# Decoder block on one core: the gate's small tensors kept in the experts' PSUM bank, with a new order of steps

## The chip, the cores and the metric

The kernel runs on one core of one Trainium2 chip. The metric is the device time of one launch in microseconds; the median of the runs counts. A core has a matrix engine (PE, which the kernel calls tensor), and the engines DVE (vector), ACT (scalar), POOL (gpsimd) and SP (sync, here the queue that issues every DMA). Each works through its own instruction stream in order; semaphores tie the streams together.

## The reference, cut to what matters

For each of 32 batch entries (256 tokens of width 256) a pre-norm decoder block is computed: a causal self-attention with 8 heads that share one key and value (part a), a cross-attention with 16 heads, a bias per head and a mask (part b), and a mixture of 8 experts with a shared one (part c):

```
    x = x + _L0_attn_ref(_layernorm(x), Wq, Wk, Wv, Wo)
    x = x + _L0_xattn_ref(_layernorm(x), ctx, ctx, bias, bias, key_mask, attn_mask, ...)
    # part c, on the layer-normed x:
    logits = einsum('btd,ed->bte', x, gate_w)
    _, idx = top_k(logits + lb_bias, 2)
    w = sigmoid(take_along_axis(logits, idx))
    w = w / (sum(w) + 1e-6)                      # two weights per token
    hidden = square(relu(einsum('nd,ehd->neh', x, w1)))
    out = sum over e of w_e * (hidden_e @ w2_e)  + shared expert
```

The gate is the part from `logits` to the two weights per token. Its tensors are tiny: 128 partitions by 2 token tiles by 8 experts.

## The kernel before

Tokens lie on 128 partitions in CT = 2 tiles. Every float32 product is made of three float16 products (high and low parts), so each result of PE is split by ACT (high part) and by DVE or POOL (low part). The work of one batch entry is cut into named steps, and each engine has its own table of steps in `ORDERS`: an entry `c_gate:0@5` means step c_gate with argument 0, for the batch entry that is 5 behind the current iteration. `iterations` walks the table once for each of 32 + LAGS iterations, so parts a, b and c of up to four entries are under way at once, and the order of a table is the order of that engine's instructions. Only the order within an engine and the semaphores matter; where a table begins does not.

Steps that the text speaks of:
- b_s:j and b_p:j, head j of part b: PE makes the scores (L1089), DVE adds the bias and takes the maximum (L829), ACT takes the exponential (L663, L665) and the high part (L673), DVE makes the low part (L836), and SP transposes both with a DMA, b_pT:j (L422), for PE's b_pv:j (L1103).
- b_comb:j on POOL (L521) adds the mask to a bias tile of 128x512 in place; b_load:p on SP brings the bias of two heads (512 KB) into one of four slots, ahead by four.
- b_store_q, b_store_k, b_stack_q, b_stack_k on SP write the split queries and keys to memory and read them back stacked for PE (16 transfers of 64 KB); b_s:0 of the next entry waits for them.
- a_s, a_n, a_pt, a_pv, a_q, a_r: scores, scaling, transposes, values, queries and reciprocals of part a.
- b_wo and c_ln: end of part b (x2) and the layer norm of part c over DVE, POOL and ACT; c_T transposes its result on PE (L993) into ps_c_hidden.
- c_f1:e and c_f2:e, e from 0 (shared) to 8: first and second product of an expert, 12 matmuls each (L966). c_f1 writes the bank ps_c_hidden; POOL squares (L535) and makes the low part (c_lo, L542). c_f2 writes the bank ps_c_out, and DVE's c_f2:e adds it to acc (L929 for e = 0, L937 with the gate's weights for the others).
- c_gate: PE writes the 16 logit columns into ps_c_out (16 matmuls of 8 columns). ACT takes exp(-logits) (L685). DVE's chain has 13 parts and 19 counted instructions, L873 to L921, each waiting on the semaphore c_gd for the one before. All of its tensors after the first read lie in SBUF (g_logits, g_biased, g_mask1 and 2, g_exp1, g_w, g_sum1). PE's c_f2:0 waits for the first of the 19 alone, since only that one reads ps_c_out; DVE's c_f2:1 waits for all 19.

Of the kernel before, what the change touches and what calls it, by code (L numbers as in the profile page):

```python
# [66 lines left out]
def order(text):  # L67
# [31 lines left out]
        a_pv:1@3 b_s:1@4 a_s:6@3 w_split:10@3 b_p:0@4 c_T:0@5 a_pt:3@3 b_s:2@4 a_pv:2@3 b_p:1@4 b_s:3@4
        c_gate:0@5 c_gate:1@5 c_gate:2@5 a_s:7@3 c_gate:3@5 c_gate:4@5 c_gate:5@5 b_p:2@4 c_gate:6@5 a_pt:4@3  # L100
        w_split:11@3 c_gate:7@5 b_s:4@4 c_f2:0@5 c_gate:8@5 c_gate:9@5 b_p:3@4 c_gate:10@5 c_gate:11@5 a_r:6@3
        a_pv:3@3 b_s:5@4 c_gate:12@5 c_f2:1@5 a_r:7@3 a_pt:5@3 b_p:4@4 b_s:6@4 a_pv:4@3 b_p:5@4 c_f2:2@5
        a_pt:6@3 b_s:7@4 b_p:6@4 b_s:8@4 a_pv:5@3 w_split:12@3 c_f2:3@5 a_pt:7@3 w_split:13@3 b_p:7@4
        w_split:14@3 w_split:15@3 a_pv:6@3 b_s:9@4 a_pv:7@3 b_p:8@4 a_ln:0@2 b_s:10@4 b_p:9@4 c_f2:4@5 a_ln:1@2
        w_split:3@2 b_p:10@4 a_wo:0@3 b_s:11@4 b_ln:0@3 b_s:12@4 b_ln:1@3 b_p:11@4 c_f2:5@5 b_s:13@4 a_T:0@2
        b_p:12@4 b_T:0@3 b_mask:0@3 w_split:4@2 a_kv:0@2 b_s:14@4 w_split:5@2 b_p:13@4 a_q:0@2 w_split:6@2
        b_s:15@4 b_p:14@4 a_q:1@2 a_s:0@2 b_r:0@4 b_p:15@4 c_f2:6@5 a_r:0@2 a_s:1@2 b_kv:0@3 a_q:2@2 a_r:1@2
        a_s:2@2 a_pt:0@2 w_split:7@2 a_s:3@2 a_r:2@2 c_f2:7@5 b_n:0@4 a_q:3@2 a_pt:1@2 b_o:0@4 a_s:4@2 a_r:3@2
        w_split:8@2 c_f2:8@5 a_s:5@2 a_pv:0@2 b_wo:0@4 a_r:4@2 w_split:9@2 c_ln:0@4 a_r:5@2 c_ln:1@4 b_s:0@3
        a_pt:2@2""",  # L110
    tensor="""
        b_s:1@4 a_pt:3@3 c_T:0@5 b_s:2@4 a_pv:2@3 a_s:7@3 c_f1:0@5 a_pt:4@3 b_s:3@4 c_gate:0@5 c_f1:1@5 a_pv:3@3
        b_s:4@4 b_pv:0@4 c_f1:2@5 c_f2:0@5 c_f1:3@5 b_s:5@4 a_pt:5@3 c_f2:1@5 c_f1:4@5 b_s:6@4 a_pv:4@3 c_f2:2@5
        b_pv:1@4 b_pv:2@4 a_pt:6@3 c_f1:5@5 b_s:7@4 a_pv:5@3 b_pv:3@4 c_f2:3@5 b_s:8@4 c_f1:6@5 a_pt:7@3 b_s:9@4
        a_pv:6@3 b_pv:4@4 c_f2:4@5 a_pv:7@3 c_f1:7@5 b_s:10@4 a_wo:0@3 b_s:11@4 b_pv:5@4 c_f2:5@5 b_s:12@4
        a_T:0@2 c_f1:8@5 b_pv:6@4 b_s:13@4 b_pv:7@4 c_f2:6@5 b_s:14@4 b_T:0@3 a_kv:0@2 b_pv:8@4 b_q:0@3 a_q:0@2
        b_pv:9@4 b_s:15@4 b_kv:0@3 a_q:1@2 b_pv:10@4 b_pv:11@4 a_s:0@2 b_kv:1@3 b_pv:12@4 a_s:1@2 b_pv:13@4
        a_q:2@2 a_pt:0@2 a_s:2@2 c_f2:7@5 a_s:3@2 a_pt:1@2 b_pv:14@4 b_pv:15@4 a_q:3@2 b_o:0@4 a_s:4@2 a_pv:0@2
# [1111 lines left out]
```

## Time and profile before

| what | value |
|---|---|
| median of 3 runs | 2490.76 us (2489.09 to 2491.76) |
| the profiled execution, its own time | 2482.43 us |
| its span, first to last instruction | 2480.6 us |
| mean granted PE clock | 0.946 of full speed |
| busy share PE, DVE, ACT, POOL | 87%, 79%, 83%, 72% |

The profile is of one execution. Busy shares are averages over the whole span, and no engine is full; what ends a stretch is read from the stretch itself, with the windows, timeline and chain views below.

### The profile page before, as it was taken

How to read it: one execution, taken by the hardware profiler on the slowest of the kernel's cores; microseconds unless marked ns; L12 is line 12 of the kernel's file. 1: busy time of each engine (PE TensorE's matmuls, PEld its weight loads, DVE VectorE, ACT ScalarE, POOL GpSimd, SP SyncE). 2: the span in 40 equal slices, each digit the busy share in tenths (PEclk: the TensorE clock that was granted, in tenths of full speed). 3: DMA queues.
4: the chain of work that ended last, by engine and by line, in shares of the span. 5: the costliest groups of instructions: out<-in, count | busy, mean ns of one | idle time of the engine just before them, and what ended most of it. 6: DMA issues, size and time to landing. Idle time of an engine off the chain costs nothing.

```text
span 2480.6 us, 73034 instructions
## 1 busy us (share of the span) xinstructions
PE 2161.2 (87%) x24128; PEld 1852.2 (75%) x24128; DVE 1964.2 (79%) x6672; ACT 2070.0 (83%) x6065; POOL 1785.0 (72%) x1899
## 2 busy tenths in 40 slices
...
GB/s 155 121 166 153 160 144 152 147 150 154 163 149 141 148 148 163 153 157 137 140 153 171 146 166 143 147 144 165 155 163 155 146 139 149 166 148 160 137 131 35
DMA packets 711784, 367.16 MB, mean 148 GB/s; under 512 B 561392, under 2 KB 659952, under 8 KB 711408
## 3 DMA queue, kind: packets, MB, share of 16 engines
...
## 4 chain that ended last, share of the span: by engine, by line
PE 52%; DVE 17%; issue 12%; ACT 12%; DMA 4%; SPq 2%; POOL 1%; DVEq 0%; ACTq 0%; POOLq 0%
PE ps_a_misc L966 12%; PE ps_c_hidden L966 11%; PE ps_c_out L966 10%; DMA b_probsT_hi_lo<-b_probs_hi_lo 4%; PE ps_a_scores L1026 4%; PE ps_b_misc L1103 3%; DVE g_weights L921 3%; PE ps_a_misc L1045 3%; PE ps_b_scores L1089 3%; ACT ps_b_probs L665 2%; DVE b_neg_scores L829 2%; ACT ps_b_probs L663 2%; PE ps_b_misc L966 2%; ACT b_probs_hi_lo L673 1%; DVE g_mask L899 1%
## 5 line engine op out<-in xcount | busy, mean ns | idle before, releaser
L521 POOL TENSOR_TENSOR bias<-bias,b_mask 128x512 f32<-128x512 f32 x512 | 648.8, 1276 | 14.6 <-DMA bias<-in_bias 13.9
L542 POOL TENSOR_TENSOR c_hidden_lo<-c_hidden,c_hidden_hi 128x512 f16<-128x512 f32 x288 | 334.2, 1161 | 228.6 <-issue 207.0
L829 DVE CUSTOM_DVE_ANT_0 b_neg_scores<-ps_b_scores,bias 128x256 f32<-128x256 f32 x1024 | 390.0, 417 | 89.5 <-PE ps_b_scores L1089 83.5
L535 POOL TENSOR_TENSOR c_hidden<-c_relu 128x512 f32<-128x512 f32 x288 | 300.2, 1042 | 207.8 <-ACT c_relu L691 197.9
L836 DVE TENSOR_TENSOR b_probs_hi_lo<-ps_b_probs,b_probs_hi_lo 128x512 f16<-128x512 f32 x512 | 349.0, 682 | 126.9 <-ACT b_probs_hi_lo L673 119.1
L663 ACT ACTIVATE ps_b_probs<-b_neg_scores,b_neg_max 128x256 f32<-128x256 f32 x512 | 245.8, 480 | 200.7 <-DVE b_probs_hi_lo L836 133.3
L966 PE MATMUL ps_c_out<-w_hi,c_hidden_hi 128*128 128x256 f16 x1152 | 321.8, 279 | 92.6 <-DVE acc L937 90.2
L966 PE MATMUL ps_c_hidden<-c_xT_hi,w_hi 128*128 128x256 f16 x1152 | 326.3, 283 | 5.7 <-DVE c_xT_lo L744 4.6
L966 PE MATMUL ps_c_hidden<-c_xT_lo,w_hi 128*128 128x256 f16 x1152 | 324.5, 282 | 0.0
L966 PE MATMUL ps_c_out<-w_hi,c_hidden_lo 128*128 128x256 f16 x1152 | 324.4, 282 | 0.0
L966 PE MATMUL ps_c_out<-w_lo,c_hidden_hi 128*128 128x256 f16 x1152 | 323.5, 281 | 0.0
L966 PE MATMUL ps_c_hidden<-c_xT_hi,w_lo 128*128 128x256 f16 x1152 | 322.8, 280 | 0.0
L673 ACT ACTIVATE b_probs_hi_lo<-ps_b_probs 128x512 f16<-128x512 f32 x512 | 303.2, 592 | 4.9 <-DMA b_probsT_hi_lo<-b_probs_hi_lo 0.4
L937 DVE SCALAR_TENSOR_TENSOR acc<-ps_c_out,g_weights,acc 128x256 f32<-128x256 f32 x512 | 222.1, 475 | 34.7 <-PE ps_c_out L966 30.0
L665 ACT ACTIVATE ps_b_probs<-b_neg_scores,b_neg_max 128x256 f32<-128x256 f32 x512 | 239.5, 468 | 0.0
L1103 PE MATMUL ps_b_misc<-b_v_hi,b_probsT_hi_lo 128*128 128x16 f16 x4096 | 220.6, 170 | 12.8 <-DMA b_probsT_hi_lo<-b_probs_hi_lo 12.4
L1103 PEld LDWEIGHTS ps_b_misc<-b_v_hi,b_probsT_hi_lo 128*128 128x128 f16 x4096 | 205.3, 97 | 20.9 <-DMA b_probsT_hi_lo<-b_probs_hi_lo 15.5
L691 ACT ACTIVATE c_relu<-ps_c_hidden 128x512 f32<-128x512 f32 x288 | 172.4, 598 | 53.6 <-PE ps_c_hidden L966 50.3
L966 PEld LDWEIGHTS ps_c_out<-w_hi,c_hidden_hi 128*128 128x128 f16 x1152 | 114.5, 99 | 122.2 <-issue 104.3
L1103 PE MATMUL ps_b_misc<-b_v_lo,b_probsT_hi_lo 128*128 128x16 f16 x2048 | 195.9, 170 | 0.0
L696 ACT ACTIVATE c_hidden_hi<-c_relu 128x512 f16<-128x512 f32 x288 | 181.4, 630 | 1.4 <-PE ps_c_out L966 1.3
L479 POOL TENSOR_TENSOR a_qT_lo<-a_qT,a_qT_hi 128x512 f16<-128x512 f32 x128 | 150.4, 1175 | 42.7 <-ACT a_qT_hi L602 42.6
...
## 6 DMA issues: line engine op xcount, KB each, us to landing
bias<-in_bias SPq DMA_DIRECT2D x256, 512.0 KB, 4.3
q_stack<-qk_scratch SPq DMA_DIRECT2D x256, 64.0 KB, 3.6
...
k_stack_even<-qk_scratch SPq DMA_DIRECT2D x128, 64.0 KB, 3.6
```

Source lines behind the costliest of these rows:

```text
L521: gp.tensor_tensor(part, part, b_mask[:, :], ALU.add).then_inc(b_c_ok, 1)
L535: gp.tensor_tensor(c_h[:, :], c_r[:, e % 2, :], c_r[:, e % 2, :], ALU.mult).then_inc(c_sq_ok, 1)
L542: gp.tensor_tensor(c_hl[:, u, :], c_h[:, :], c_hh[:, u, :], ALU.subtract).then_inc(c_h_ok, 1)
L663: act.activation(ps_bp[:, 0:T], b_t[:, u, 0, :], ACT.Exp, bias=b_mx[:, u, 0:1], scale=-1.0, accum_out=b_sum[:, 0, j:j + 1])
L665: act.activation(ps_bp[:, T:2 * T], b_t[:, u, 1, :], ACT.Exp, bias=b_mx[:, u, 1:2], scale=-1.0, accum_out=b_sum[:, 1, j:j + 1]).then_inc(b ...
L673: act.activation(b_p2[:, j % DEPTH, :, 0, :], ps_bp[:, :].rearrange("p (c t) -> p c t", c=CT), ACT.Copy).then_inc(b_ph_ok, 1)
L696: act.activation(c_hh[:, e % 2, :], c_r[:, e % 2, :], ACT.Square).then_inc(c_hh_ok, 1)
L829: last = dve.tensor_tensor_reduce(out=b_t[:, u, c, :], in0=ps_bs[:, c * T:(c + 1) * T], in1=bias[:, slot, at:at + T], scale=-2.0, scalar=3 ...
L836: dve.tensor_tensor(b_p2[:, j % DEPTH, :, 1, :], ps_bp[:, :].rearrange("p (c t) -> p c t", c=CT), b_p2[:, j % DEPTH, :, 0, :], ALU.subtrac ...
L937: last = dve.scalar_tensor_tensor(out=acc[:, c, :], in0=ps_c2[:, c * D:(c + 1) * D], scalar=g_we[:, c, e - 1:e], in1=acc[:, c, :], op0=ALU ...
L966: last = pe.matmul(out, stat(s, k), mov(m, k), start=(k == 0 and n == 0), stop=(k == chunks - 1 and n == len(parts) - 1))
L1103: last = pe.matmul(ps_bm[:, at:at + BD], b_pT[:, u, c, part, s, :], v[:, s, j * BD:(j + 1) * BD], start=(s == 0 and n == 0), stop=(s == CT ...
```

## The change

Five of the gate's tensors move from SBUF into columns of ps_c_out behind the logits: exp1 (1 + exp), first and both (the masks), chosen (masks times sigmoid) and total (sum + 1e-6). The biased logits come straight from PSUM in one instruction in place of two, so GATE_STEPS goes from 19 to 18. No instruction of the gate on DVE then reads two tensors from SBUF, and the single-source ones on small tensors have their source or their result in PSUM, but for the cast of the indices. Since PE's c_f2:0 writes over that bank, it now waits for all 18 steps. All five tables of ORDERS are new.

```
-        GATE_STEPS = 19
+        GATE_STEPS = 18
...
+                logits, exp1, first, both, chosen = [
+                    ps_c2[:, n * CT * NE:(n + 1) * CT * NE].rearrange("p (c e) -> p c e", c=CT) for n in range(5)]
+                total = ps_c2[:, 5 * CT * NE:5 * CT * NE + CT]
...
-                    for c in range(CT):
-                        dve.tensor_tensor(g_sel[:, c, :], g_lg[:, c, :], lb[:, :], ALU.add).then_inc(c_gd, 1)
+                    dve.scalar_tensor_tensor(out=g_sel[:, :, :], in0=logits, scalar=1.0 / W_UP,
+                                             in1=lb[:, None, :].to_broadcast([P, CT, NE]), op0=ALU.mult,
+                                             op1=ALU.add).then_inc(c_gd, 1)
...
-                    dve.tensor_scalar(g_e1[:, :, :], g_ex[:, :, :], 1.0, None, ALU.add).then_inc(c_gd, 1)
+                    dve.tensor_scalar(exp1, g_ex[:, :, :], 1.0, None, ALU.add).then_inc(c_gd, 1)
...
-                        dve.tensor_scalar(g_m1[:, c, :], iota, g_idf[:, c, 0:1], None,
-                                          ALU.is_equal).then_inc(c_gd, 1)
+                        dve.tensor_scalar(first[:, c, :], iota, g_idf[:, c, 0:1], None, ALU.is_equal).then_inc(c_gd, 1)
...
-                    dve.tensor_tensor(g_w[:, :, :], g_m2[:, :, :], g_sg[:, :, :], ALU.mult).then_inc(c_gd, 1)
+                    dve.tensor_tensor(chosen, both, g_sg[:, :, :], ALU.mult).then_inc(c_gd, 1)
...
-                    dve.tensor_scalar(g_s1[:, :], g_s[:, :], 1e-6, None, ALU.add).then_inc(c_gd, 1)
+                    dve.tensor_scalar(total, g_s[:, :], 1e-6, None, ALU.add).then_inc(c_gd, 1)
...
-                        last = dve.tensor_scalar(g_we[:, c, :], g_w[:, c, :], g_si[:, c:c + 1], 1.0 / (W_UP * H_UP),
+                        last = dve.tensor_scalar(g_we[:, c, :], chosen[:, c, :], g_si[:, c:c + 1], 1.0 / (W_UP * H_UP),
...
                 if e == 0:
-                    pe.wait_ge(c_gd, after(b, GATE_STEPS, 1))
+                    pe.wait_ge(c_gd, after(b, GATE_STEPS, GATE_STEPS))
```

Of the tables, the lines of PE's after the change that hold its order from c_gate to c_f2:2:

```
+        b_s:0@3 b_s:1@3 a_pv:2@2 b_s:2@3 c_T:0@4 a_pt:4@2 b_s:3@3 c_f1:0@4 c_gate:0@4 a_pv:3@2 c_f1:1@4 b_s:4@3
+        b_pv:0@3 a_pt:5@2 c_f1:2@4 b_pv:1@3 b_s:5@3 a_pv:4@2 c_f1:3@4 a_pt:6@2 c_f2:0@4 b_s:6@3 c_f1:4@4
+        b_pv:2@3 a_pv:5@2 c_f2:1@4 b_s:7@3 c_f1:5@4 a_pt:7@2 c_f2:2@4 b_s:8@3 b_pv:3@3 a_pv:6@2 b_pv:4@3
```

In the table before, PE has c_f1:1, a_pv:3, b_s:4, b_pv:0 and c_f1:2 between c_gate:0 and c_f2:0. In the new one it has a_pv:3, c_f1:1, b_s:4, b_pv:0, a_pt:5, c_f1:2, b_pv:1, b_s:5, a_pv:4, c_f1:3 and a_pt:6.

The second half of the gate on DVE before the change; ps_b_scores, ps_b_probs and ps_a_misc belong to the attention parts, and the row of g_weights (L921) comes right behind these:

```order
L929 SCALAR_TENSOR_TENSOR acc<-ps_c_out,x 128x512
L908 TENSOR_TENSOR g_w<-g_mask,g_sigmoid 128x16
L911 TENSOR_REDUCE g_sum<-g_w 128x2
L836 TENSOR_TENSOR b_probs_hi_lo<-ps_b_probs,b_probs_hi_lo 128x2x256
L914 TENSOR_SCALAR g_sum<-g_sum 128x2
L917 RECIPROCAL g_inv<-g_sum 128x2
L799 RECIPROCAL a_inv<-a_sum 128x2
L774 TENSOR_TENSOR a_oT_lo<-ps_a_misc,a_oT_hi 128x256
L829 ISA b_neg_scores,b_neg_max<-ps_b_scores,bias 128x256
L829 ISA b_neg_max 128x1
L829 ISA b_neg_scores,b_neg_max<-ps_b_scores,bias 128x256
L829 ISA b_neg_max 128x1
```

The same place after the change:

```order
L909 TENSOR_REDUCE g_sum<-ps_c_out 128x2
L912 TENSOR_SCALAR ps_c_out<-g_sum 128x2
L915 RECIPROCAL g_inv<-ps_c_out 128x2
L794 RECIPROCAL a_inv<-a_sum 128x2
L919 TENSOR_SCALAR g_weights<-ps_c_out,g_inv 128x8 x2
L824 ISA b_neg_scores,b_neg_max<-ps_b_scores,bias 128x256
L824 ISA b_neg_max 128x1
L824 ISA b_neg_scores,b_neg_max<-ps_b_scores,bias 128x256
L824 ISA b_neg_max 128x1
L831 TENSOR_TENSOR b_probs_hi_lo<-ps_b_probs,b_probs_hi_lo 128x2x256
L927 SCALAR_TENSOR_TENSOR acc<-ps_c_out,x 128x512
```

The first accumulation (acc from ps_c_out and x) stood ahead of the gate's end and now stands behind it, and fewer attention steps stand between the gate's last parts.

SP at the end of a batch entry's part b, before the change, from the store of the queries on:

```order
L369 DMA bias<-in_bias 128x1024
L389 DMA qk_scratch<-b_qT_hi_lo 128x4x256
L422 DMA_TRANSPOSE b_probsT_hi_lo<-b_probs_hi_lo 128x8x128
L430 DMA key_padding<-in_pad 128x64
L382 DMA qk_scratch<-b_kT_hi_lo 128x4x256
L422 DMA_TRANSPOSE b_probsT_hi_lo<-b_probs_hi_lo 128x8x128
L414 DMA q_stack<-qk_scratch 16x8x256 x8
L403 DMA k_stack_even<-qk_scratch 16x8x256 x4
L403 DMA k_stack_odd<-qk_scratch 16x8x256 x4
```

The same place after the change:

```order
L384 DMA qk_scratch<-b_qT_hi_lo 128x4x256
L364 DMA bias<-in_bias 128x1024 x4
L417 DMA_TRANSPOSE b_probsT_hi_lo<-b_probs_hi_lo 128x8x128
L377 DMA qk_scratch<-b_kT_hi_lo 128x4x256
L417 DMA_TRANSPOSE b_probsT_hi_lo<-b_probs_hi_lo 128x8x128
L409 DMA q_stack<-qk_scratch 16x8x256 x8
L398 DMA k_stack_even<-qk_scratch 16x8x256 x4
L398 DMA k_stack_odd<-qk_scratch 16x8x256 x4
```

Four loads of bias (b_load:6, 7, 5 and 4) now stand together ahead of the last two transposes and the stacks, where one stood; the load of the padding row has gone elsewhere.

PE between the second head of part b and the second half of its fourth, around c_T, before the change:

```order
L1089 MATMUL ps_b_scores<-k_stack_odd,q_stack 128x256 x2
L1033 MATMUL ps_a_probsT<-constants,a_probs 128x128
L1034 MATMUL ps_a_probsT<-constants,a_probs 128x128
L1035 MATMUL ps_a_probsT<-constants,a_probs 128x128
L993 MATMUL ps_c_hidden<-constants,c_xn 128x128 x4
L1089 MATMUL ps_b_scores<-k_stack_even,q_stack 128x256 x2
```

And after it:

```order
L1087 MATMUL ps_b_scores<-k_stack_even,q_stack 128x256 x2
L991 MATMUL ps_c_hidden<-constants,c_xn 128x128 x4
L1031 MATMUL ps_a_probsT<-constants,a_probs 128x128
L1032 MATMUL ps_a_probsT<-constants,a_probs 128x128
L1033 MATMUL ps_a_probsT<-constants,a_probs 128x128
L1087 MATMUL ps_b_scores<-k_stack_odd,q_stack 128x256 x2
L964 MATMUL ps_c_hidden<-c_xT_hi,w_hi 128x256
```

Between c_T and the first expert product PE had b_s:2, a_pv:2 and a_s:7; now it has a_pt:4 and b_s:3 there.

## Rows read from the trace of the kernel before

**Rows 1.** The page: busy time, and the chain that ended last by engine.

```profile
PE 2161.2 (87%) x24128; PEld 1852.2 (75%) x24128; DVE 1964.2 (79%) x6672; ACT 2070.0 (83%) x6065; POOL 1785.0 (72%) x1899
...
PE 52%; DVE 17%; issue 12%; ACT 12%; DMA 4%; SPq 2%; POOL 1%; DVEq 0%; ACTq 0%; POOLq 0%
```

**Rows 2.** Windows: busy PE, PEld, DVE, ACT, POOL; PE clock; nine gate stretches, their sum.

```profile
1217.66:1227.66 10.00, 6.66 (x59) 5.21 (x58) 9.80 (x27) 6.73 (x22) 8.10 (x8) 1.00 0.32 68
...
sum 90.00, PE 59.58 PEld 46.44 DVE 87.81 ACT 60.52 POOL 72.84; mean PE 6.62 PEld 5.16 DVE 9.76 ACT 6.72 POOL 8.09
```

**Rows 3.** Timeline of DVE in one gate: start us, duration us, instruction.

```profile
1220.37 0.90 DVE L908 TENSOR_TENSOR g_w<-g_mask,g_sigmoid 128x16 f32<-128x16 f32 x1
...
1221.39 0.68 DVE L836 TENSOR_TENSOR b_probs_hi_lo<-ps_b_probs,b_probs_hi_lo 128x512 f16<-128x512 f32 x1
1221.99 0.51 DVE L914 TENSOR_SCALAR g_sum<-g_sum 128x2 f32<-128x2 f32 x1
...
1222.68 0.40 DVE L774 TENSOR_TENSOR a_oT_lo<-ps_a_misc,a_oT_hi 128x256 f16<-128x256 f32 x1
1223.00 0.41 DVE L829 CUSTOM_DVE_ANT_0 b_neg_scores<-ps_b_scores,bias 128x256 f32<-128x256 f32 x1
...
1223.68 2.27 DVE L921 TENSOR_SCALAR g_weights<-g_w,g_inv 128x8 f32<-128x8 f32 x2
```

**Rows 4.** Timeline of POOL in the same stretch.

```profile
1220.20 1.04 POOL L535 TENSOR_TENSOR c_hidden<-c_relu 128x512 f32<-128x512 f32 x1
1221.32 1.16 POOL L542 TENSOR_TENSOR c_hidden_lo<-c_hidden,c_hidden_hi 128x512 f16<-128x512 f32 x1
...
1224.66 1.26 POOL L521 TENSOR_TENSOR bias<-bias,b_mask 128x512 f32<-128x512 f32 x1
```

**Rows 5.** Groups of DVE's gate instructions: busy us, mean ns; last row min/median/max ns, first and last start.

```profile
L921 DVE TENSOR_SCALAR g_weights<-g_w,g_inv 128x8 f32<-128x8 f32 x64 | 69.8, 1133 | 0.0
L899 DVE TENSOR_SCALAR g_mask<-constants,g_idx_f 128x8 f32<-128x8 f32 x64 | 35.0, 590 | 0.0
L908 DVE TENSOR_TENSOR g_w<-g_mask,g_sigmoid 128x16 f32<-128x16 f32 x32 | 28.2, 881 | 0.0
L891 DVE TENSOR_SCALAR g_exp<-g_exp 128x16 f32<-128x16 f32 x32 | 19.5, 608 | 13.5 <-ACT g_exp L685 13.4
L914 DVE TENSOR_SCALAR g_sum<-g_sum 128x2 f32<-128x2 f32 x32 | 16.7, 522 | 0.0
...
L873 DVE TENSOR_SCALAR g_logits<-ps_c_out x32: 168/169/175, 177.0 to 2449.2; 128x16 f32<-128x16 f32 x32
```

**Rows 6.** The chain that ended last, pieces of PE: start us, us.

```profile
1195.71 0.49 PE ps_a_scores L1026 x6
...
1229.16 0.16 PE ps_a_probsT L1033
...
1229.54 1.31 PE ps_c_hidden L966 x12
1230.85 0.22 PE ps_b_scores L1089 x2
...
1231.57 0.28 PE ps_b_misc L1103 x12
```

**Rows 7.** Windows as in rows 2: stretches ahead of nine gates (12 us); one behind.

```profile
sum 108.00, PE 80.36 PEld 61.75 DVE 83.32 ACT 85.12 POOL 42.42; mean PE 8.93 PEld 6.86 DVE 9.26 ACT 9.46 POOL 4.71
...
1300.02:1322.02 22.00, 22.00 (x241) 19.51 (x239) 16.95 (x57) 18.93 (x53) 15.35 (x18) 0.92 0.77 156
```

**Rows 8.** Timelines of SP's queue and PE before a first head; the bias load's landing.

```profile
1258.38 0.57 SPq L369 DMA_DIRECT2D bias<-in_bias  x1
...
1264.42 3.95 SPq L414 DMA_DIRECT2D q_stack<-qk_scratch  x8
...
1276.08 0.38 PE L1089 MATMUL ps_b_scores<-k_stack_even,q_stack 128*128 128x256 f16 x2 [0.33 <-issue]
...
bias<-in_bias SPq DMA_DIRECT2D x256, 512.0 KB, 4.3
```

More of the change, by code:

```diff
@@ L81 @@
+        b_pT:7@4 b_pT:9@4 a_T:0@2 b_pT:10@4 b_pT:12@4 b_pT:11@4 b_pT:13@4 b_store_q:0@3 b_load:6@4 b_load:7@4
+        b_load:5@4 b_load:4@4 b_pT:14@4 b_store_k:0@3 b_pT:15@4 b_stack_q:0@3 b_stack_k:0@3 b_pT:0@3 b_load:0@3
+        b_pT:1@3 b_load:1@3 c_f2:8@5 b_pT:2@3""",
     gpsimd="""
-        b_v:0@4 b_comb:5@4 a_q:3@3 b_comb:6@4 c_ln:0@5 b_res:0@4 c_f1:0@5 c_lo:0@5 c_f1:1@5 c_lo:1@5 b_kv:0@3
-        c_f1:2@5 c_lo:2@5 b_comb:7@4 c_f1:3@5 b_comb:8@4 c_lo:3@5 b_comb:9@4 c_f1:4@5 c_lo:4@5 c_f1:5@5 c_lo:5@5
@@ L98 @@
-    vector="""
[L99 to L110, printed above, removed]
@@ L111 @@
-    tensor="""
[L112 to L118, printed above, removed]
-        c_f2:8@5 a_s:5@2 b_wo:0@4 a_pt:2@2 a_pv:1@2 a_s:6@2 b_s:0@3""",
+        c_ln:0@5 b_comb:2@4 b_comb:3@4 b_comb:4@4 b_v:0@4 b_comb:5@4 c_f1:0@5 b_res:0@4 c_lo:0@5 c_f1:1@5
```

89 lines of the change are left out of this document (50 added, 39 removed).

## The prediction, made before the changed kernel ran

> **What bounds the kernel now.** I read the page first. No engine is full: PE is busy 87% of the span, ACT 83%, DVE 79%, and the chain that ended last is 52% PE, 17% DVE, 12% ACT [rows 1]. So the bound changes from stretch to stretch. Counting the starts of the gate's first DVE instruction, 32 of them from 177.0 to 2449.2 us [rows 5], one batch entry takes (2449.2 - 177.0) / 31 = 73.3 us. I then cut nine entries by the windows view, each relative to that first instruction. In the ten microseconds from 4 to 14 us behind it the picture is the same in all nine: DVE is busy 9.76 of 10, while PE is busy 6.62, ACT 6.72 and POOL 8.09 [rows 2]. DVE alone bounds this stretch, and PE stands idle for 3.4 us and ACT for 3.3 us of it. Elsewhere PE bounds: it is busy all of 22.00 us in the stretch behind the gate shown in [rows 7]. Ahead of the gate there is another hole, which DVE does not fill either (PE busy 8.93 of 12, DVE 9.26, POOL 4.71 [rows 7]): there the layer norm c_ln goes round DVE, POOL and ACT.
>
> What fills DVE in the gate stretch are tiny instructions that take long. g_weights handles 8 columns in 1133 ns on average, while the read of the logits, 16 columns from PSUM, takes 169 ns [rows 5]. The timelines side by side say why. L908 ends at 1220.37 + 0.90 = 1221.27, and POOL's L535 had ended at 1221.24. L914 ends at 1222.50, POOL's L542 at 1222.48. The two of L921 end at 1225.95, POOL's L521 at 1225.92 [rows 3, 4]. Each of these waits until the running POOL instruction is over, and ends some 0.03 us behind it; meanwhile DVE's whole queue stands behind it. The instruction of 128x512 next to them, L836, reads one SBUF tensor and one PSUM tensor, and takes 0.68 us beside a busy POOL without any such stretch [rows 3].
>
> **What the change removes.** With 169 ns as the length of such an instruction when nothing holds it, the excess over 32 entries is: L921 69.8 - 64 x 0.17 = 58.9 us; L899 35.0 - 10.9 = 24.1; L908 28.2 - 5.4 = 22.8; L891 19.5 - 5.4 = 14.1; L914 16.7 - 5.4 = 11.3 [rows 5]. Together 131.2 us, or 4.1 us per entry. The instruction saved in the biased logits is one of that same small size. I call it nothing.
>
> Three of the five (L891, L899, L914) will read SBUF and write PSUM, and no DVE instruction of the trace does that. The bounds are 0.17 us as for the read from PSUM, and their present length, which would keep 24.1 + 14.1 + 11.3 = 49.5 us of the excess, 1.5 us per entry. I take the low end, since the row nearest to them (L873, the same operation with PSUM on the other side) has it. The Trainium skill ("VectorE: DVE Perf Modes", What auto-detection actually checks) says that the two-port mode is taken when the single source and the destination both lie in SBUF. No run here shows yet that a destination in PSUM is enough; by that rule the low end holds, and with the high end the forecast would be some 46 us later.
>
> The other two, and the reductions and masks, now read PSUM. The row for that is L873, 168 to 175 ns in all 32 [rows 5], so I price it at nothing. The Trainium skill ("VectorE: DVE Perf Modes", The TRN2 errata) gives a fixed part of 120 cycles from PSUM against 58 from SBUF at 0.96 GHz, 65 ns more each; for nine such reads that is an estimate of 0.6 us per entry, 18 us in all, and it speaks against this change. The forecast would be 2425 by it.
>
> **What it is worth.** DVE loses 4.1 us of work in a stretch where it was the bound by 3.3 us, the idle time of ACT, next after it. So 3.3 us is the most that this stretch gives per entry. POOL idles 1.9 us there and 7.3 us in the stretch ahead [rows 2, 7]; the new POOL order puts b_comb:1 to b_comb:5 ahead of the first expert's square, where it was idle, so I don't count it as a limit.
>
> **What it adds.** PE's c_f2:0 now waits for the whole gate. Behind it on PE stand b_s:6, c_f1:4 and everything that follows; ACT's c_sq:2, POOL's c_lo:2 and DVE's c_f2:0 wait for it in turn. On PE between c_gate and c_f2:0 lie, by [rows 6], three c_f1 at 1.31, two a_pv at 0.50 (1231.07 to 1231.57, between b_scores' end and b_misc), two a_pt at 0.38 (1229.16 to 1229.54), two b_s at 0.22, two b_pv at 0.3: 6.7 us. On DVE the 18 steps are at most 18 x 0.17 = 3.1 us when free, and between them stand two b_p at 0.60, one b_s at 0.68 (1223.00 to 1223.68), one a_pv at 0.32, one a_pt at no more than b_p's 0.60, two reciprocals at 0.17 [rows 3, 5]: 3.1 us, together 6.2 us. The wait is covered by 0.5 us. If the gate were still held by POOL, it would be 6.2 + 4.1 = 10.3 us against 6.7, a stall of 3.6 us for every engine, about as much as PE idles now.
>
> **What moves.** Between c_T and c_f1:0 PE had b_s, a_pv and a_s (0.22 + 0.50 + 0.49 [rows 6]) and has a_pt and b_s (0.38 + 0.22). The way from c_T through ACT and DVE is not shorter, so I charge 0.6 us of new idle time on PE. Ahead of b_s:0, where PE waits for the stacked keys, PE gets c_f2:6, a_pt:3 and a_s:7 and gives a_q:1 away: 1.31 + 0.38 + 0.5 - 1.31 = 0.9 us more cover. On SP three more bias loads stand ahead of the stacks. Their issue alone is 3 x 0.57 = 1.7 us; if each held the queues for its whole time to landing, it would be 3 x 4.3 = 12.9 us [rows 8]. Before, PE waited 0.33 us at this place in the entry shown. I take the issue end, since bias loads are issued throughout while other transfers land, and of it 0.9 is covered by PE; the rest of 0.8 I set against the fact that SP waits for b_p:14 anyway. Net nothing.
>
> **The sum.** 3.3 - 0.6 = 2.7 us per entry, times 31 periods = 84 us. The profiled execution took 2482.4 us (1.8 more than its span), so 2398 on its scale; the median of the runs stands 8.3 us above it, so 2407.
>
> **Rivals.**
> - More than that (15%). In [rows 7] the granted clock behind the gate is 0.92, with PE busy all the time, after PE's idle time in the gate. Six of nine entries showed 0.92 or 0.93 there, which costs 0.08 x 22 = 1.8 us each, 1.2 on average. If PE no longer idles, this goes too, and if the hole ahead of the gate does not grow: 3.3 + 1.2 = 4.5 us, 140 us, 2351.
> - Part of it is lost again (20%). The gate ends later than c_f2:0 by a microsecond, because exp(-logits) comes late from ACT or b_p waits inside the gate, or three of the five keep their length (1.5 us). Then 1 to 1.5 us per entry, 31 to 47 us: 2445 to 2460.
> - The change doesn't do what it says (5%). The instructions still wait for POOL, for another reason than two SBUF tensors. The stall is then at c_f2:0 instead of in DVE's queue, 3.6 against 3.4 us: 2490 to 2500. Against it: L836 beside a busy POOL.
> - Slower (10%), by one mechanism: the burst of bias loads makes the stacks late. It decides from the point where they come later than 2.7 us of gain plus 0.9 of cover, 3.6 us. With a delay halfway between 1.7 and 12.9, 7.3 us, the entry is 3.7 us longer, 115 us: about 2605; at 5 us it is 1.4 us, 2534. For it: the stacks are already what PE waits for. Against it: only 0.33 us.
>
> **How the numbers follow.** The forecast of 2407, with 2380 to 2440 around it, holds 50%. With 15% for more, 20% for less and 5% + 10% for the last two, faster by over 0.2% is 0.85, within 0.2% (about what this measurement can tell) 0.05, slower 0.10. The range of 2350 to 2470 takes in the forecast, most of the first rival and all of the second.
>
> **What would show it.** Right: g_weights' two near 0.2 us each and none of the gate's instructions ending with a POOL instruction; DVE under 9 of 10 us in the gate stretch and PE near full there; a period near 70.6 us; PE's idle time before c_f2:0 under 0.5 us. Wrong: PE idle before c_f2:0 for the gate's last step by more than 1 us, PE idle before b_s:0 for the stacks by more than 1.5 us, or the instructions that write PSUM still at 0.5 us or more.

## The result, and the profile after the change

The median went from 2490.76 to 2469.91 us (2468.02 to 2475.79 over five runs), a ratio of 0.9923 (95% interval 0.9907 to 0.994). Of the five runs of the kernel before, four took 2487.29 to 2491.76 us; one took 4171.51 us and is left out of the ratio. The change makes the kernel 21 us faster where 84 were forecast. The median lies just inside the upper end of the range, and that is luck: a gain that I had too small makes up for half of a loss that I had overlooked (see the part on why).

The page of the kernel after the change, busy time and chain, as in [rows 1]:

```profile
PE 2161.8 (88%) x24128; PEld 1865.0 (76%) x24128; DVE 1862.6 (75%) x6640; ACT 2078.2 (84%) x6065; POOL 1780.3 (72%) x1899
...
PE 59%; ACT 17%; DMA 10%; issue 7%; DVE 3%; SPq 3%; POOL 1%; ACTq 0%; DVEq 0%; POOLq 0%
```

DVE fell from 17% of the chain to 3%, and DMA rose from 4% to 10%. Where each happens, the windows show. Below are, after the change, the stretches from 24 to 13, from 13 to 1 us ahead of the gate's first DVE instruction and from 4 to 14 us behind it: the first of nine entries, then the sum of the nine (columns as in [rows 2]; PE's clock is the third number from the end).

```profile
380.12:391.12 11.00, 7.46 (x77) 6.48 (x76) 6.04 (x22) 5.79 (x19) 6.65 (x6) 0.84 1.26 151
...
sum 99.00, PE 70.23 PEld 59.09 DVE 49.91 ACT 48.49 POOL 51.39; mean PE 7.80 PEld 6.57 DVE 5.55 ACT 5.39 POOL 5.71
391.12:403.12 12.00, 8.88 (x69) 6.61 (x68) 10.75 (x41) 11.78 (x40) 7.27 (x9) 0.86 0.51 62
...
sum 108.00, PE 74.35 PEld 53.76 DVE 91.80 ACT 101.97 POOL 64.10; mean PE 8.26 PEld 5.97 DVE 10.20 ACT 11.33 POOL 7.12
408.12:418.12 10.00, 9.97 (x114) 8.90 (x112) 8.82 (x32) 9.87 (x28) 8.98 (x8) 1.00 0.73 149
...
sum 90.00, PE 89.77 PEld 79.88 DVE 78.50 ACT 88.60 POOL 81.18; mean PE 9.97 PEld 8.88 DVE 8.72 ACT 9.84 POOL 9.02
```

The last of the three answers to [rows 2]: PE 9.97 of 10 in place of 6.62. The first is new. Before the change these 11 us were full:

```profile
sum 99.00, PE 96.07 PEld 86.11 DVE 84.26 ACT 90.85 POOL 89.60; mean PE 10.67 PEld 9.57 DVE 9.36 ACT 10.09 POOL 9.96
```

Now every engine idles there together, PE for 3.2 us, ACT for 5.6, DVE for 5.5, and the granted clock (a mean over the window), 1.00 in all nine before, was 0.69 in seven of nine. What they wait for stands in the groups of PE's matmuls (by form; the last number is PE's idle time ahead of the group over the whole span, with its releasers), first before the change, then after:

```profile
L966 PE MATMUL ps_c_hidden<-c_xT_hi,w_hi 128*128 128x256 f16 x1152 | 326.3, 283 | 5.7 <-DVE c_xT_lo L744 4.6 <-ACT c_relu L691 1.2
L966 PE MATMUL ps_c_out<-w_hi,c_hidden_hi 128*128 128x256 f16 x1152 | 321.8, 279 | 92.6 <-DVE acc L937 90.2 <-POOL c_hidden_lo L542 1.4 <-DVE acc L929 0.6
L1103 PE MATMUL ps_b_misc<-b_v_hi,b_probsT_hi_lo 128*128 128x16 f16 x4096 | 220.6, 170 | 12.8 <-DMA b_probsT_hi_lo<-b_probs_hi_lo 12.4
L1089 PE MATMUL ps_b_scores<-k_stack_even,q_stack 128*128 128x256 f16 x512 | 104.0, 287 | 42.2 <-issue 23.8 <-DVE b_neg_max L829 18.3
L1089 PE MATMUL ps_b_scores<-k_stack_odd,q_stack 128*128 128x256 f16 x512 | 100.0, 277 | 56.2 <-DVE b_neg_max L829 56.1
```

```profile
L964 PE MATMUL ps_c_hidden<-c_xT_hi,w_hi 128*128 128x256 f16 x1152 | 326.3, 283 | 32.2 <-DVE c_xT_lo L739 27.4 <-ACT c_relu L686 3.7
L964 PE MATMUL ps_c_out<-w_hi,c_hidden_hi 128*128 128x256 f16 x1152 | 318.9, 277 | 9.7 <-POOL c_hidden_lo L537 4.6 <-DVE acc L935 3.6
L1101 PE MATMUL ps_b_misc<-b_v_hi,b_probsT_hi_lo 128*128 128x16 f16 x4096 | 225.6, 170 | 107.6 <-DMA b_probsT_hi_lo<-b_probs_hi_lo 107.4
L1087 PE MATMUL ps_b_scores<-k_stack_odd,q_stack 128*128 128x256 f16 x512 | 102.7, 284 | 43.7 <-DVE b_neg_max L824 43.6
L1087 PE MATMUL ps_b_scores<-k_stack_even,q_stack 128*128 128x256 f16 x512 | 99.4, 276 | 19.8 <-DVE b_neg_max L824 14.9 <-issue 4.8
```

PE's busy time plus its idle time is the span, so these rows make a ledger that closes. The third column is experiment e4 below; "rest" is the span less the lines above it.

| us over the span | before | after | e4 |
|---|---|---|---|
| PE busy | 2161.2 | 2161.8 | 2112.7 |
| idle before c_f2 (ps_c_out) | 92.6 | 9.7 | 9.1 |
| idle before b_pv (ps_b_misc) | 12.8 | 107.6 | 8.8 |
| idle before b_s, both parities | 98.4 | 63.5 | 64.5 |
| idle before c_T | 35.8 | 32.5 | 31.9 |
| idle before c_f1's first product | 5.7 | 32.2 | 31.3 |
| rest | 74.1 | 60.3 | 60.4 |
| span | 2480.6 | 2467.6 | 2318.7 |

The change took 82.9 us from the wait before c_f2 and 34.9 from those before b_s, and gave 94.8 us to the wait of b_pv for its transposed probabilities, which had been no wait to speak of, and 26.5 to c_f1's first product. A row tells where PE waits, and not which part of the change moved it; e2 below shows that for the first of them. The landing times (page, DMA issues: KB each, median us) of the loads and of the store of the keys that stands between the last two transposes:

```profile
bias<-in_bias SPq DMA_DIRECT2D x256, 512.0 KB, 4.7
...
qk_scratch<-b_kT_hi_lo SPq DMA_DIRECT2D x32, 256.0 KB, 6.7
```

That store took 3.7 us before, now 6.7. One such place on SP's queue, and the wait on PE behind it (timelines; for PE the bracket is the idle time and its releaser):

```profile
1247.43 3.42 SPq L364 DMA_DIRECT2D bias<-in_bias  x4
1250.95 1.46 SPq L417 DMA_TRANSPOSE b_probsT_hi_lo<-b_probs_hi_lo  x1
1252.54 0.69 SPq L377 DMA_DIRECT2D qk_scratch<-b_kT_hi_lo  x1
1253.33 3.68 SPq L417 DMA_TRANSPOSE b_probsT_hi_lo<-b_probs_hi_lo  x1
...
1260.36 0.19 PE L1101 MATMUL ps_b_misc<-b_v_hi,b_probsT_hi_lo 128*128 128x16 f16 x1 [2.12 <-DMA b_probsT_hi_lo<-b_probs_hi_lo]
```

The last transpose is issued at 1253.33 and its matmuls start at 1260.36, 7 us later. The four loads ahead of it bring 2 MB. The three transposes issued from 1245 to 1266 us took 6.8 us to land (median); in like stretches of e4 and e9 below it is 3.7 and 3.4 us.

### The profile page after: what moved, and what is told of

Its sections match the earlier page's. It is cut to its first block, busy times and chain, and to the rows that moved or that the text cites. A ratio compares the mean times of both kernels' runs of the same rounds, so it can differ in the third digit from the quotient of the medians.

```text
span 2467.6 us, 73004 instructions
## 1 busy us (share of the span) xinstructions
PE 2161.8 (88%) x24128; PEld 1865.0 (76%) x24128; DVE 1862.6 (75%) x6640; ACT 2078.2 (84%) x6065; POOL 1780.3 (72%) x1899
## 2 busy tenths in 40 slices
DMA packets 711784, 367.16 MB, mean 149 GB/s; under 512 B 561392, under 2 KB 659952, under 8 KB 711408
## 4 chain that ended last, share of the span: by engine, by line
PE 59%; ACT 17%; DMA 10%; issue 7%; DVE 3%; SPq 3%; POOL 1%; ACTq 0%; DVEq 0%; POOLq 0%
PE ps_c_hidden L964 18%; PE ps_c_out L964 13%; PE ps_a_misc L964 11%; DMA b_probsT_hi_lo<-b_probs_hi_lo 10%; PE ps_b_misc L1101 4%; PE ps_b_scores L1087 3%; ACT ps_b_probs L658 3%; PE ps_a_misc L1043 3%; ACT ps_b_probs L660 2%; PE ps_a_scores L1024 2%; PE ps_a_misc L1044 1%; ACT b_probs_hi_lo L668 1%; ACT a_probs L603 1%; SPq L417 1%; ACT c_xn L569 1%
## 5 line engine op out<-in xcount | busy, mean ns | idle before, releaser
L964 PE MATMUL ps_c_hidden<-c_xT_hi,w_hi 128*128 128x256 f16 x1152 | 326.3, 283 | 32.2 <-DVE c_xT_lo L739 27.4
L530 POOL TENSOR_TENSOR c_hidden<-c_relu 128x512 f32<-128x512 f32 x288 | 300.0, 1042 | 73.4 <-ACT c_relu L686 58.8
L1101 PE MATMUL ps_b_misc<-b_v_hi,b_probsT_hi_lo 128*128 128x16 f16 x4096 | 225.6, 170 | 107.6 <-DMA b_probsT_hi_lo<-b_probs_hi_lo 107.4
L964 PE MATMUL ps_c_out<-w_lo,c_hidden_hi 128*128 128x256 f16 x1152 | 317.8, 276 | 0.0
L964 PE MATMUL ps_c_out<-w_hi,c_hidden_lo 128*128 128x256 f16 x1152 | 317.5, 276 | 0.0
L618 ACT ACTIVATE a_probsT_hi<-ps_a_probsT 128x384 f16<-128x384 f32 x256 | 126.4, 494 | 144.4 <-PE ps_a_probsT L1033 144.3
L454 POOL TENSOR_TENSOR c_ve<-c_mv,eps 128x2 f32<-128x2 f32 x32 | 6.2, 194 | 280.3 <-DVE c_mv L732 280.3
```

The lines of the kernel that those rows point to most:

```text
L530: gp.tensor_tensor(c_h[:, :], c_r[:, e % 2, :], c_r[:, e % 2, :], ALU.mult).then_inc(c_sq_ok, 1)
L964: last = pe.matmul(out, stat(s, k), mov(m, k), start=(k == 0 and n == 0), stop=(k == chunks - 1 and n == len(parts) - 1))
L1101: last = pe.matmul(ps_bm[:, at:at + BD], b_pT[:, u, c, part, s, :], v[:, s, j * BD:(j + 1) * BD], start=(s == 0 and n == 0), stop=(s == CT ...
```

## The experiments

All times are medians; "before" was run again on each chip: 2484.63 us for e1 to e4, 2486.35 for e5 to e8, 2486.82 for e9. With the 2490.76 us above it differs by 6 us from chip to chip, so a difference between runs of two chips is good to about that; e1 to e4 compare best with each other, and so do e5 to e8.

**e1: the four loads spread out.** The changed kernel, SP's table alone edited:

```
- a_ln:0@3 b_pT:8@4 b_pT:7@4 b_pT:9@4 a_T:0@2 ... b_pT:11@4 b_pT:13@4 b_store_q:0@3
- b_load:6@4 b_load:7@4 b_load:5@4 b_load:4@4 b_pT:14@4
+ a_ln:0@3 b_load:4@4 b_pT:8@4 b_pT:7@4 b_pT:9@4 b_load:5@4 a_T:0@2 ... b_pT:11@4 b_load:6@4 b_pT:13@4
+ b_store_q:0@3 b_load:7@4 b_pT:14@4
```

> The changed kernel with one edit: on SP, b_load:4, 5 and 6 stand between the transposes b_pT:6 and b_pT:13 again, so that one bias load instead of four stands ahead of the last two transposes. The changed kernel lost 2.7 us of PE time per entry in the 11 us that begin 24 us ahead of the gate, behind transposes that took 6.8 us (median of the three in that stretch) to land. Theory 1, the burst of four loads makes those transposes late: they land in about 4 us, the hole closes by 2 to 3.5 us per entry, and the time falls by 60 to 110 us, to 2360 to 2410. Theory 2, PE, ACT and DVE simply reach the last heads in an order that leaves no cover for a transpose, whatever else is loaded: the hole stays at 2 us or more and the time at 2455 to 2475. Theory 3, moving the loads back delays the transposes in the middle of the entry instead: PE waits there, and the time stays within 20 us of 2470.

Measured 2339.04 us, ratio 0.9411 [0.939, 0.9433]: 131 us below the changed kernel, more than the 60 to 110 of theory 1. PE's wait for the transposes fell from 107.6 to 18.9 us. The burst is the cause, and it cost more than I gave it.

**e2: the gate of before with the new tables.** The five tensors back in SBUF, c_f2:0 waiting for one step again; all tables as after the change.

> The gate as before the change (all its tensors in SBUF, 19 steps, PE's c_f2:0 waiting for the first of them alone) with the new tables of steps. If the moved tensors saved 3.3 us per entry in the gate stretch and the new tables cost the rest, this kernel has the loss without the gain: 2470 + 31 x 3 to 3.5 = 2560 to 2580. If the new tables alone would have hidden the slow gate (DVE has less beside it there), it stays within 30 us of 2470. The long instructions (g_weights 1.1 us) should be back in both cases, and PE's wait of about 3.5 us is then for DVE's c_f2:0.

Measured 2539.35 us, 1.0229 [1.0205, 1.0254]: 55 us slower than before and 69 us slower than the whole change. So the new tables alone lose, and the gate's edit is worth 69 us beside them. Neither theory had this number; it lies between them. The groups of PE:

```profile
L966 PE MATMUL ps_c_out<-w_hi,c_hidden_hi 128*128 128x256 f16 x1152 | 319.2, 277 | 6.0 <-DVE acc L937 3.8 <-POOL c_hidden_lo L542 2.3
L1103 PE MATMUL ps_b_misc<-b_v_hi,b_probsT_hi_lo 128*128 128x16 f16 x4096 | 225.5, 170 | 107.1 <-DMA b_probsT_hi_lo<-b_probs_hi_lo 106.8
```

The wait for the transposes is all there (107.1 us) without the new gate. The wait before c_f2 is gone too (6.0 us), which the last sentence of the expectation had wrong: with the slow gate in the new tables, PE waits for DVE before a_pt (45.0 us, 4.0 in the changed kernel) and b_s (86.7 us, there 63.5) instead. So the row of c_f2 in the ledger is the tables' doing, and the gate's worth is read from the spans: PE's idle time is 374.9 us here and 305.8 in the changed kernel, 69.1 less, at the same busy time.

**e3: the new gate with the tables of before.** In DVE's table c_gate:12 goes ahead of a_r:6 and c_f2:0 behind b_s:5, so that c_f2:0 stands behind the gate's end; in PE's, three more steps lie ahead of c_f2:0:

```
DVE + c_gate:11 c_gate:12 a_r:6 a_pv:3 b_s:5 c_f2:0 c_f2:1
PE  - c_f1:2 c_f2:0 c_f1:3 b_s:5 a_pt:5 c_f2:1 c_f1:4
PE  + c_f1:2 c_f1:3 b_s:5 a_pt:5 c_f2:0 c_f1:4 c_f2:1
```

> The gate in PSUM, 18 steps, with the tables of before. DVE's c_gate:12 goes ahead of b_s:5 and its c_f2:0 behind it, and on PE c_f2:0 and c_f2:1 go two and one expert products later, since c_f2:0 has to wait for the whole gate. Theory 1 (the gate's gain is whole, the new tables lost most of it on SP): 3.3 us less per entry, less up to 1 us for c_f2:0 reached after 5.5 us of PE work with 6 us of gate on DVE: 2 to 3.3 us per entry, 2390 to 2430. Theory 2 (any order gives the gain back, since PE then arrives earlier at transfers that take as long as before): 2455 to 2480.

Measured 2485.42 us, 0.9994 [0.9973, 1.0015]: no difference from before. Theory 1 missed by 55 us or more. Theory 2 missed by 5, and its reason is not what happened: PE's wait for the transposes (13.8 us) and the part of b_s's wait without a releaser (27.4) stayed near those of before (12.8 and 23.8). DVE was relieved (5.63 of 10 us in the gate stretch), but PE rose only to 7.17. Its groups show why:

```profile
L963 PE MATMUL ps_c_hidden<-c_xT_hi,w_hi 128*128 128x256 f16 x1152 | 325.8, 283 | 74.0 <-ACT c_relu L685 71.1 <-DVE c_xT_lo L738 2.9
L963 PE MATMUL ps_c_out<-w_hi,c_hidden_hi 128*128 128x256 f16 x1152 | 315.5, 274 | 68.0 <-DVE g_weights L918 36.9 <-DVE acc L934 27.9 <-POOL c_hidden_lo L536 2.0
```

c_f2:0 now waits for g_weights (36.9 us), and ACT's c_sq:2, which waits for that same product, holds ACT's c_relu late, for which c_f1 waits in turn: 71.1 us, where it was 1.2.

**e4: two loads among the transposes, two behind the stacks.** As e1, but

```
- b_pT:11@4 b_load:6@4 b_pT:13@4 b_store_q:0@3 b_load:7@4 b_pT:14@4 b_store_k:0@3 b_pT:15@4
+ b_pT:11@4 b_pT:13@4 b_store_q:0@3 b_pT:14@4 b_store_k:0@3 b_pT:15@4
- b_stack_q:0@3 b_stack_k:0@3 b_pT:0@3
+ b_stack_q:0@3 b_stack_k:0@3 b_load:6@4 b_load:7@4 b_pT:0@3
```

> As e1_loads_spread, but b_load:6 and b_load:7 go behind the 16 stack transfers, so that no bias load stands between b_store_q and the last two transposes. Theory 1 makes the transposes faster still: 0 to 20 us below e1_loads_spread. If the loads are then too late for POOL's b_comb:4 of the next entry, POOL waits for them, and it is slower than e1_loads_spread.

Measured 2318.93 us (2315.76 to 2320.98), 0.9337 [0.9319, 0.9356]. This version beats both kernels, by 166 us the one before and by 151 us the changed one, and e1 by 20, the most that was expected. Its chain by engine:

```profile
PE 77%; ACT 12%; issue 7%; DVE 2%; DMA 1%; POOL 1%; SPq 0%; ACTq 0%; DVEq 0%; POOLq 0%
```

The stretch from 24 to 13 us ahead of nine gates, windows as above:

```profile
sum 99.00, PE 98.79 PEld 89.70 DVE 88.80 ACT 95.25 POOL 90.24; mean PE 10.98 PEld 9.97 DVE 9.87 ACT 10.58 POOL 10.03
```

And the group of b_pv:

```profile
L1101 PE MATMUL ps_b_misc<-b_v_hi,b_probsT_hi_lo 128*128 128x16 f16 x4096 | 220.0, 170 | 8.8 <-DMA b_probsT_hi_lo<-b_probs_hi_lo 8.8
```

The hole is closed, the clock there is 1.00 in all nine, and the ledger says where the 148.9 us between the two spans come from: 98.8 from b_pv's wait, 49.1 from PE's busy time, the rest from elsewhere. The 49.1 us are the same 24128 matmuls at a mean granted clock of 0.960 instead of 0.938 (2161.8 x 0.938 / 0.960 = 2112.3, measured 2112.7).

**e5: the kernel before, with three loads together.** The same fault put into the kernel before the change:

```
- b_load:7@5 b_store_q:0@4 b_pT:14@5
+ b_store_q:0@4 b_load:6@5 b_load:7@5 b_load:5@5 b_pT:14@5
```

b_load:5 and b_load:6 are taken from their places among b_pT:8 to b_pT:12.

> The kernel before with one edit on SP: b_load:5 and b_load:6 move from the middle of the entry to between b_store_q and b_pT:14, beside b_load:7, so three bias loads stand together ahead of the last two transposes (b_load:4 can't join them in these tables, since POOL would wait for it ahead of the queries that SP waits for). If loads standing together are what costs, this alone makes the kernel before slower: with four of them the changed kernel lost 2.7 us of PE and more by the clock per entry, and spreading three of them gave back 131 us. Here PE reaches the last heads later relative to their transposes, so less: 30 to 100 us above 2485. If the burst costs only together with the new order on PE, within 15 us of 2485.

Measured 2588.69 us, 1.0415 [1.0389, 1.044]: 102 us slower, just above the 30 to 100 expected. PE's wait for the transposes rose from 12.8 to

```profile
L1103 PE MATMUL ps_b_misc<-b_v_hi,b_probsT_hi_lo 128*128 128x16 f16 x4096 | 223.7, 171 | 96.3 <-DMA b_probsT_hi_lo<-b_probs_hi_lo 96.0
```

so three loads do it nearly as well as four, with no other part of the change present. The keys' store lands 5.8 us after its issue here, where it was 3.7.

**e6: e4 with the gate of before.**

> The kernel of e4_loads_last_two_behind_stacks with the gate of before (SBUF, 19 steps, c_f2:0 waiting for the first). Measured against it, this is the worth of the gate in tables whose SP order does no harm. If the gate's worth is the 2.2 to 3.3 us per entry of the gate stretch whatever SP does: 2319 + 68 to 105 = 2387 to 2424. If the slow gate is worth less once SP's hole is gone (something else then ends the entry): under 2370. If it is worth more, since PE's idle time also lowers its clock: over 2430.

Measured 2407.74 us, 0.9686 [0.9659, 0.9713]: 88.8 us above e4, 2.9 us for each of 31 periods, inside the 68 to 105 expected. This is the gate's worth with the burst out of the way. By the profiled spans (2414.8 and 2318.7 us) the difference is 56.8 us of PE's idle time, 1.8 per period, and 39.3 of its busy time (2152.0 against 2112.7), at a mean granted clock of 0.946 against 0.960. As in e2, the wait is not where it was before the change: c_f2 waits only 8.0 us, and the steps that share DVE's queue with the gate wait instead.

```profile
L1033 PE MATMUL ps_a_probsT<-constants,a_probs 128*128 128x128 f32 x256 | 77.5, 303 | 21.5 <-DVE a_probsT_lo L767 20.3 <-ACT a_probs L617 1.3
...
L1045 PE MATMUL ps_a_misc<-a_probsT_hi,a_v_hi 128*128 128x256 f16 x256 | 72.1, 282 | 37.3 <-DVE a_oT_lo L774 36.0
```

**e7: e4 with the layer norm c_ln ahead of b_p:0 on ACT.** The hole just ahead of the gate is left in e4 (PE 8.60 of 12).

```
ACT - w_split:11@2 b_p:0@3 c_ln:0@4 a_pv:2@2 b_s:1@3 c_T:0@4 b_p:1@3
ACT + w_split:11@2 c_ln:0@4 b_p:0@3 a_pv:2@2 c_T:0@4 b_s:1@3 b_p:1@3
```

> The kernel of e4_loads_last_two_behind_stacks with two edits in ACT's table: c_ln:0 ahead of b_p:0, and c_T:0 ahead of b_s:1. In its trace c_ln started 1.1 us after POOL's last step for it, behind b_p:0, and PE stood idle for 0.94 us ahead of c_T and 1.08 us ahead of the first expert product. If ACT's order is what PE waits for there: 0.5 to 1.2 us less per entry, 2282 to 2304. If b_p:0, which is then later, or the scores of the second head take over the wait: 2310 to 2335.

Measured 2326.56 us, 0.9352 [0.9325, 0.9379]: no gain over e4, from which it can't be told (8 us above it, with intervals that overlap). The first theory fell; the second, that b_p:0 or the scores of the second head take over the wait, gave 2310 to 2335, and the groups bear it out:

```profile
L964 PE MATMUL ps_c_hidden<-c_xT_hi,w_hi 128*128 128x256 f16 x1152 | 328.4, 285 | 17.2 <-DVE c_xT_lo L739 13.4 <-ACT c_relu L686 3.8
L1087 PE MATMUL ps_b_scores<-k_stack_odd,q_stack 128*128 128x256 f16 x512 | 103.9, 287 | 84.8 <-DVE b_neg_max L824 84.8
L991 PE MATMUL ps_c_hidden<-constants,c_xn 128*128 128x128 f32 x128 | 24.5, 322 | 13.7 <-ACT c_xn L569 13.6
```

Against e4's 31.3, 44.1 and 31.9, the two waits that c_ln causes lost 32 us together, and the wait of the odd heads for b_neg_max gained 41. Putting one of two urgent steps of ACT first only changes which of them PE waits for.

**e8: e3 with ACT's c_sq:2 later,** from behind b_p:3 to behind a_pt:5, where the product that it needs is due:

```
ACT - b_p:3@3 c_sq:2@4 c_f1:3@4 a_s:7@2 b_s:4@3 a_pt:5@2 b_p:4@3
ACT + b_p:3@3 c_f1:3@4 a_s:7@2 b_s:4@3 a_pt:5@2 c_sq:2@4 b_p:4@3
```

> The kernel of e3_new_gate_old_orders (new gate, tables of before) with one edit in ACT's table: c_sq:2 goes from behind b_p:3 to behind a_pt:5, since it waits for c_f2:0, which now waits for the whole gate; in its trace ACT stood idle for 3.1 us on it, with a relu and two heads behind it that PE needed. If the gain of the new gate was lost to this queue behind the new wait: 1 to 3 us per entry less, 2390 to 2455. If PE's own wait for the gate's last step (1.2 us in that trace) and the later c_f2 chain are what took it: within 20 us of 2485.

Measured 2434.53 us, 0.9784 [0.9758, 0.9809]: one step moved on one engine gives 51 us. The wait for c_relu fell:

```profile
L963 PE MATMUL ps_c_hidden<-c_xT_hi,w_hi 128*128 128x256 f16 x1152 | 322.1, 280 | 34.3 <-ACT c_relu L685 30.4 <-DVE c_xT_lo L738 3.9
```

That is inside the 2390 to 2455 expected. c_f2's own wait stayed (67.4 us). In the new tables it is 9.7 us, with more work between c_gate and c_f2:0; that such work alone would take it away in the old ones too was not run.

**e9: the changed kernel with loads of a quarter.** SP's order is untouched; b_load:4 to 7 bring 256 of the 1024 columns, and the rest of those bias tiles is left out.

```
- sp.dma_start(bias[:, p % SLOTS, :], bias_d[b * PAIRS + q])
+ sp.dma_start(bias[:, p % SLOTS, 0:256], bias_d[b * PAIRS + q][:, 0:256])
```

> The changed kernel, its order untouched, with the four bias loads that stand together (b_load:4 to 7) each bringing 256 of 1024 columns, 128 KB in place of 512 KB. It leaves out the rest of those loads, so half of the heads use stale bias values. The number of transfers and SP's instructions are the same. If it is the bytes in front of the last two transposes that make them late, the hole closes as it did when the loads were spread: 2470 less 90 to 160 us, 2310 to 2380. If it is SP's time to issue four more transfers (some 2.5 us for the four), or the waits ahead of them in SP's queue, the time stays above 2430.

Measured 2320.15 us, 0.9323 [0.9298, 0.9349]: 150 us below the changed kernel, the same as e4, with every DMA issued in the same place of the queue. PE's wait for the transposes:

```profile
L1101 PE MATMUL ps_b_misc<-b_v_hi,b_probsT_hi_lo 128*128 128x16 f16 x4096 | 220.0, 170 | 9.4 <-DMA b_probsT_hi_lo<-b_probs_hi_lo 9.3
```

SP's timeline at such a place:

```profile
1246.73 2.90 SPq L364 DMA_DIRECT2D bias<-in_bias  x4
1249.73 1.25 SPq L417 DMA_TRANSPOSE b_probsT_hi_lo<-b_probs_hi_lo  x1
...
1251.90 1.29 SPq L417 DMA_TRANSPOSE b_probsT_hi_lo<-b_probs_hi_lo  x1
```

The four loads still take 2.90 us to issue, where the full ones took 3.42, and of the two transposes behind them the first takes 1.25 in place of 1.46, the last 1.29 in place of 3.68. It is the bytes ahead of the transposes, not SP's time to issue the loads, nor the order as such. The fewer bytes over the whole run (318.40 MB in place of 367.16) are no rival: e4 moves all of them and is as fast.

## Why the prediction was right in direction and wrong in size

**The total: two errors that partly cancel.** Without the burst the change gains 166 us (e4), twice the forecast of 84; the burst takes some 150 of them back (151 between e4 and the changed kernel), for which the forecast had nothing.

**What the change removes: right.** The five groups priced at 131.2 us of excess went from 169.2 us of busy time [rows 5] to 38.8, 130.4 less. DVE's whole busy time fell by less, 101.6, since others grew, the cast by 7.5 us and b_mask by 6.4 among them. After the change, DVE's groups:

```profile
L919 DVE TENSOR_SCALAR g_weights<-ps_c_out,g_inv 128x8 f32<-128x8 f32 x64 | 11.5, 222 | 0.1
L898 DVE TENSOR_SCALAR ps_c_out<-constants,g_idx_f 128x8 f32<-128x8 f32 x64 | 11.3, 222 | 0.0
L906 DVE TENSOR_TENSOR ps_c_out<-ps_c_out,g_sigmoid 128x16 f32<-128x16 f32 x32 | 5.6, 173 | 0.0
L912 DVE TENSOR_SCALAR ps_c_out<-g_sum 128x2 f32<-128x2 f32 x32 | 5.2, 164 | 1.1
L890 DVE TENSOR_SCALAR ps_c_out<-g_exp 128x16 f32<-128x16 f32 x32 | 5.2, 162 | 0.0
```

A result in PSUM is enough: L912 and L890 read SBUF and write PSUM in 0.16 us, the low end that I took. The added reads from PSUM cost nothing that shows: L906 takes 173 ns, and the same operations, from SBUF before and from PSUM now, took 170 and 165 (the sum), 165 and 171 (the reciprocal g_inv), 246 and 245 ns (the reciprocal g_sigmoid). So the 65 ns more for each that the Trainium skill ("VectorE: DVE Perf Modes", The TRN2 errata) would give, which had the forecast at 2425, do not appear in these rows.

**What it is worth: right, a little less.** "3.3 us is the most": measured 2.9 us per period with the rest of the tables good (e6 against e4), 2.2 (69 us) beside the burst (e2). But the 3.3 were meant as idle time, and of the 2.9 some 1.8 are; the rest is busy time, most of it by the clock (2152.0 x 0.946 / 0.960 = 2120.6, measured 2112.7), for which this term had no place. And the idle time that I read in the gate stretch belongs to the old tables: in e6, with the slow gate in the new ones, PE is busy 7.95 of 10 us there, not 6.62.

**The wait of c_f2:0: right.** "Covered by 0.5 us" holds in the new tables; g_weights releases none of the 9.7 us. In the old ones the same wait cost all of the gain (e3). The cover is in the tables, and this is why the two parts of the change belong together.

**c_T's cover: about right.** "I charge 0.6 us": the idle time before c_f1's first product rose by 26.5 us, 0.9 per period, and that before c_T fell by 0.1.

**The stacks' cover: right.** "0.9 us more cover": the part of b_s's wait without a releaser in the profile fell from 23.8 to 4.8 us, 0.6 per period. The stacks are not late. Setting this gain to nothing was too low, and the 0.33 us of the entry shown were too little to go by: over the span it was 0.8 per period.

**The step that failed: "Their issue alone is 3 x 0.57 = 1.7 us ... I take the issue end ... Net nothing."** Two things were wrong in it. The price: what counts here are the bytes queued ahead, not the time that SP takes to issue the loads. The keys' store behind the burst lands 3.0 us later than before (6.7 against 3.7), between my two bounds of 1.7 and 12.9, and e9 saves half a microsecond of issue and gets the whole loss back. And the victim: I asked only whether the stacks would be late. Between the burst and the stacks stand b_pT:14 and b_pT:15, the last two transposes, and PE had not the work to cover their delay: at the place shown it stood idle for 0.70 us before the first b_pv behind the burst and for 2.12 before the second. The ledger puts 94.8 us there, 3.1 per period, against a charge of nothing. My tenth for "slower" had the right burst, the wrong place, and so never the right price. The Trainium skill ("DMA: Bandwidth & Descriptors", Queues, rings and completion order) says that SP's DMAs share one ring on each DMA engine, and that the engine consumes a ring's descriptors in order: a transpose issued behind four loads stands behind their bytes. The trace agrees (the keys' store, 3.7 to 6.7 us), and by that rule the place to look was the next transfer on the queue.

**The clock: the first rival, turned round.** I gave 15% to the granted clock behind the gate rising from 0.92. It did: 1.00 from 14 to 36 us behind the gate's start in all nine entries. But the new hole, in which PE idles, came with 0.69 to 0.84 in eight of nine, and PE's busy time did not fall (2161.2 to 2161.8). Without the hole both gains show: e4 has 48.5 us less PE time than before, and 113.4 us less idle time, where 84 were forecast. The mean clock (0.946 to 0.960) accounts for 31.5 of the 48.5; the rest stays open. The 29 beyond the forecast are about what the waits before b_s lost (98.4 to 64.5). That is why the fixed version lies below the forecast of 2407, and below the rival's 2351.

**The signs that I set.** None of the three for "wrong" came: PE's idle time before c_f2:0 is at most 0.3 us per period, that before b_s:0 for the stacks 0.2, and the instructions that write PSUM take 0.16 to 0.22. Each watched a place that was fine, and none the transposes. Of those for "right", the lengths of g_weights (0.22 us), DVE (8.72 of 10) and PE (9.97) in the gate stretch came. The period did not: 72.7 us, where 73.3 were to fall to 70.6. And one of the gate's instructions still ends with POOL's, the cast of the last section.

Still open is the hole just ahead of the gate, 3.4 us of PE per entry in e4; e7 shows that moving c_ln on ACT alone doesn't close it. Whether three loads or four are needed for the full loss wasn't separated from the other differences between e5 and the changed kernel.
